# Local transformer: ScalarE lays the masks in PSUM, copies both halves of the turned probabilities and scales the MLP's rows

## What is computed

```python
qkv = x @ Wqkv                       # q, k, v, 16 heads x 64
q = l2norm(q) * qs; k = l2norm(k) * ksc
q = q * cos * scale + rotate_half(q) * sin * scale        # k likewise
mask = (it < jb) | (it > jb + w) | (jb == -1)
sim = einsum('bhwie,bhwje->bhwij', bq, bk2) * 8
attn = softmax(where(mask, -max, sim), -1)
x = x + (attn @ bv2) @ Wo            # then the MLP on shifted, normed rows:
x = x + (a * gelu(gate)) @ W2 + b2   # a, gate = norm(shifted x) @ W1 + b1
```

## Time and profile before

| | |
|---|---|
| median of 3 runs | 2441.62 us (2440.64 to 2445.67) |
| the profiled execution | 2439.11 us, of which the span is 2437.3 us |
| stretch of the 96 steps | about 540 to 2140 us of the span |
| busy in that stretch of 1600 us | PE 1532, DVE 1377, ACT 979, POOL 956 us |
| TensorE clock granted | 0.968 of full speed over all, 1.00 in that stretch |
| a half-layer with its MLP | about 137 us, e.g. 1176 to 1313 us |

### The profile page before, as it was taken

One profiled execution on the slowest core, in us unless ns is written; L12 is line 12 of the kernel. 1 busy time (PEld: TensorE's weight loads), 2 busy tenths in 40 slices (PEclk: granted clock), 3 DMA queues, 4 the chain that ended last, 5 costly groups with the idle time before them and its releaser, 6 DMA issues.

```text
span 2437.3 us, 83769 instructions
## 1 busy us (share of the span) xinstructions
PE 2257.1 (93%) x36453; PEld 1530.4 (63%) x36453; DVE 1855.8 (76%) x4174; ACT 1298.4 (53%) x2414; POOL 1154.0 (47%) x855
## 2 busy tenths in 40 slices
PE   8999899889999999999999999999999999979985
PEld 4567554446667666666667676666766676655564
DVE  5742588779988889798888889897888888756612
ACT  3524154355666666656566666656566666525332
POOL 1037300046666556565656556565656556410064
PEclk8989899899999999999999999999999999999898
DMA  9012200000111211121101211021111111130012
GB/s 297 31 31 41 59 1 1 5 27 20 41 29 37 68 33 31 35 68 37 42 20 37 69 45 33 20 68 37 42 26 31 33 46 33 34 109 2 21 37 77
DMA packets 63736, 106.92 MB, mean 44 GB/s; under 512 B 11700, under 2 KB 48831, under 8 KB 56844
## 3 DMA queue, kind: packets, MB, share of 16 engines
q1 hardware_dynamic: 57626, 93.00, 13.5%
q0 software_dynamic: 4736, 8.29, 1.7%
q10 hardware_dynamic: 1010, 0.29, 0.1%
HBM read 42.55 MB, written 13.24 MB: 23 GB/s over the span
## 4 chain that ended last, share of the span: by engine, by line
PE 62%; POOL 12%; DVE 11%; issue 10%; ACT 3%; DMA 2%; SPq 0%; POOLq 0%; ACTq 0%; DVEq 0%
PE ps L2213 10%; PE ps L2316 6%; PE ps L2295 5%; POOL mem L3007 5%; PE ps L2257 4%; PE ps L2234 4%; PE ps L2222 4%; PE ps L2272 3%; POOL mem L3020 3%; PE ps L2382 3%; PE ps L2368 2%; PE ps L2359 2%; PE ps L1196 2%; POOL mem L3014 2%; PE ps L1682 2%
## 5 line engine op out<-in xcount | busy, mean ns | idle before, releaser
L3007 POOL TENSOR_TENSOR mem<-mem 128x512 f32<-128x512 f32 x384 | 571.6, 1495 | 557.2 <-DVE mem L2524 554.0
L2213 PE MATMUL ps<-mem 128*128 128x512 f32 x768 | 380.8, 608 | 8.6 <-ACT mem L2811 3.4
L2839 ACT ACTIVATE mem<-ps 128x512 f32<-128x512 f32 x384 | 221.5, 603 | 155.7 <-PE ps L2234 155.1
L2818 ACT ACTIVATE mem<-ps 128x512 f32<-128x512 f32 x384 | 220.6, 597 | 144.1 <-PE ps L2213 107.3
L2519 DVE TENSOR_TENSOR mem<-ps,mem 128x512 f32<-128x512 f32 x384 | 258.5, 673 | 13.0 <-ACT mem L2818 13.0
L2524 DVE TENSOR_TENSOR mem<-ps,mem 128x512 f32<-128x512 f32 x384 | 261.2, 680 | 0.0
L2234 PEld LDWEIGHTS ps<-mem 128*128 128x128 f32 x1536 | 183.2, 142 | 114.9 <-issue 96.2
L2295 PEld LDWEIGHTS ps<-mem 64*64 64x64 f32 x12288 | 191.7, 135 | 79.7 <-issue 77.5
L2531 DVE TENSOR_REDUCE mem<-mem 128x16 f32<-128x1024 f32 x192 | 232.0, 1208 | 0.0
L3020 POOL TENSOR_TENSOR mem<-mem 128x1024 f32<-128x1024 f32 x95 | 180.7, 1902 | 82.0 <-DVE mem L2592 82.0
L2234 PE MATMUL ps<-mem 128*128 128x128 f32 x1536 | 212.0, 274 | 5.9 <-DVE mem L2564 3.1
(11 more groups left out here) (313 smaller groups left out, 4154.6 us busy)
## 6 DMA issues: line engine op xcount, KB each, us to landing
mem<-mem SPq DMA_DIRECT2D x48, 768.0 KB, 5.8
mem<-in_Wqkv SPq DMA_DIRECT2D x6, 1536.0 KB, 6.7
mem<-mem SPq DMA_DIRECT2D x36, 256.0 KB, 3.5
y<-mem SPq DMA_DIRECT2D x8, 512.0 KB, 6.2
mem<-in_W12T SPq DMA_DIRECT2D x8, 512.0 KB, 7.7
mem<-y SPq DMA_DIRECT2D x16, 256.0 KB, 4.9
mem<-in_L3W SPq DMA_DIRECT2D x16, 256.0 KB, 5.6
mem<-in_L2Wo SPq DMA_DIRECT2D x6, 512.0 KB, 7.0
```

The costliest lines, as they stand in the source:

```text
L2213: e.matmul(self.K.ps[:, o, :], self.columns(u, bb), self.K.l2[l % 2]["Wqkv"][:, 512 * i:512 * i + 512], start=True, stop=True, skip_group_ ...
L3007: e.tensor_tensor(t1[:, cols], t1[:, cols], self.T2[:, cols], ALU.add).then_inc(s("rotated"), 1)
```

## The change

The two mask matmuls of each step are gone. ACT writes the masks into banks 3 and 2 instead, with two copies (`a_mask`) during the step before; PE waits for a counter `seeds` and its score matmuls add onto what lies there. The transposes into bank 3 keep the same instruction with other accumulation flags. `a_mask` waits, for bank 3, until ACT's own copy of the transposes is done, and for bank 2 until DVE has read the third quarter of the rotation of `g + 3` (`rotated_half`). The second half of the turned probabilities is copied by ACT right behind the first, in 93 of 96 steps. The MLP's eight tiles of rows are scaled by ACT (`a_rows`) in 11 of 12 half-layers, between the second transposes' copy and the turn; DVE computes only the bias for it. The counter `bias_parts` of an earlier stage is now called `seeds` too.

```diff
-    BESIDE_ACT = {..., (1, 2): (("turn", 0),), ...}
+    BESIDE_ACT = {..., (1, 2): (("rows", 0), ("turn", 0)), ...}
@@ pe_by_feature
-            last = e.transpose(ps[:, o, 128 * c:128 * c + 128], self.T1[r % 2][k][:, h:h + 128], self.K.ident)
+            last = e.matmul(ps[:, o, 128 * c:128 * c + 128], self.T1[r % 2][k][:, h:h + 128], self.K.ident, start=c == 0,
+                            stop=True, is_transpose=True, skip_group_check=True)
@@ pe_scores
-        mask = self.K.maskb[:, 1 if u % 4 == 0 and g % 2 else 0, :]
         banks = self.SCORES
-        for odd in range(2):
-            after(e, self.freed[banks[odd]])
-            e.matmul(ps[:, banks[odd], :], self.K.identb, mask, start=True, stop=False, skip_group_check=True)
+        e.wait_ge(*s.at("seeds", 2 * g + 2))
@@ v_turned_p
+        if self.scalar_copies(g):        # g + 3 < self.NG
+            return
@@ v_norm
-        for i in range(8):
-            j = 8 * bp + i
-            e.tensor_scalar(K.XN[:, i, :], K.XN[:, i, :], K.mv[:, j, 0:1], K.rs[:, j:j + 1], ALU.subtract,
-                            ALU.mult).then_inc(s("mlp_rows"), 1)
+        if f + 1 < self.NF:
+            c = slice(8 * bp, 8 * bp + 8)
+            e.scalar_tensor_tensor(K.rt[:, c], K.mv[:, c, 0], -1.0, K.rs[:, c], ALU.mult, ALU.mult).then_inc(s("x_centred"), 1)
+        else:
+            ...
@@ scalar, even steps
                     self.a_by_feature(e, g + 2, 1)
                 if this:
+                    self.a_mask(e, g + 1, 1)
+                    self.a_mask(e, g + 1, 0)
                     self.a_beside(e, hl, w, 3)
@@ scalar, odd steps
                     self.a_values(e, u + 1, 3)
                 if placed:
+                    self.a_mask(e, g + 1, 0)
+                    self.a_mask(e, g + 1, 1)
+                if placed:
                     self.a_by_feature(e, g + 2, 2)
@@ new
+    def a_mask(self, e, g, odd):
+        K, s = self.K, self.s
+        if odd == 0:
+            if g + 1 < self.NG:
+                e.wait_ge(*s.at("placed", 4 * (g + 1) + 2))
+            else:
+                e.wait_ge(*s.at("lessened", 2 * g - 1))
+        elif g + 2 < self.NG:
+            e.wait_ge(*s.at("rotated_half", 4 * (g + 2) + 3))
+        else:
+            e.wait_ge(*s.at("lessened", 2 * g))
+        e.activation(K.ps[:, self.SCORES[odd], :], K.maskb[:, 1 if g % 8 == 1 else 0, :], ACT.Copy).then_inc(s("seeds"), 1)
+
+    def a_rows(self, e, f):
+        K, s = self.K, self.s
+        e.wait_ge(*s.at("x_centred", f + 3))
+        for i in range(8):
+            j = 8 * (f % 2) + i
+            e.activation(K.XN[:, i, :], K.XN[:, i, :], ACT.Identity, bias=K.rt[:, j:j + 1], scale=K.rs[:, j:j + 1]
+                         ).then_inc(s("mlp_rows"), 1)
@@ a_turned_p
+        if self.scalar_copies(g):
+            e.wait_ge(*s.at("p_turned", 2 * g + 2))
+            e.activation(view(self.PT[:, 1], "p c b h q -> p (c b h q)"), ps[:, self.TURN_P[1], :], ACT.Copy
+                         ).then_inc(s("p_cols_too"), 1)
```

More of the change, by code:

```diff
@@ L1467 @@
     LEAD = 3
-    TOTALS = dict(weight_sums=2, weight_totals=1, first_weights=1, second_weights=1, tap_rows=32, taps=3, bias_parts=1,
+    TOTALS = dict(weight_sums=2, weight_totals=1, first_weights=1, second_weights=1, tap_rows=32, taps=3, seeds=1,
                   normed=NT, ready_rows=NT, rows_turned=B, cols=B, up=NT, hidden_rows=NT, rounded=NT, rounded_turn=NT, cols2=NT,
@@ L1532, in v_steps @@
         e.wait_ge(v.sem, t)
-        e.tensor_copy(self.parts.bitcast(BF16)[three, 0:512], rest[three]).then_inc(s("bias_parts"), 1)
+        e.tensor_copy(self.parts.bitcast(BF16)[three, 0:512], rest[three]).then_inc(s("seeds"), 1)
         yield
@@ L1645, in tensor @@
         e.wait_ge(*s.at("taps", 3))
-        e.wait_ge(*s.at("bias_parts", 1))
+        e.wait_ge(*s.at("seeds", 1))
         for i in range(self.LEAD):
@@ L1967 @@
                   (5, 0): (("gate", 1),), (5, 2): (("down", 1),)}
-    BESIDE_ACT = {(1, 0): (("shift", 0),), (1, 1): (("guess", 0),), (1, 2): (("turn", 0),), (1, 3): (("turn", 1),),
+    BESIDE_ACT = {(1, 0): (("shift", 0),), (1, 1): (("guess", 0),), (1, 2): (("rows", 0), ("turn", 0)), (1, 3): (("turn", 1),),
                   (2, 2): (("gelu", 0),), (4, 1): (("turn_x", 0),), (4, 3): (("gelu", 1),), (6, 0): (("turn_x", 1),)}
     BESIDE_POOL = {(0, 0): (("kept", 0),), (4, 1): (("tables", 0),)}
-    TOTALS = dict(cleared=5, kept=32, kept_late=32, x_normed=NT, x_centred=2, x_turned=2 * NF, x_cols=4 * NF, tables=6 * DEPTH, qk=4 * NG, squared=4 * NG,
+    TOTALS = dict(cleared=5, kept=32, kept_late=32, x_normed=NT, x_centred=NF + 1, x_turned=2 * NF, x_cols=4 * NF, tables=6 * DEPTH, qk=4 * NG, squared=4 * NG,
                   guessed=NG, mlp_variance=NF, mlp_guessed=NF,
@@ L1975 @@
                   p_cols=NG, p_cols_too=NG, values_mm=4 * NU, values=4 * NU, values_shifted=16 * (2 * NU - NF),
-                  weighed=2 * NG, out_cols=2 * NG, projected=NU, attention_added=NU, shift_mm=NF, mlp_shifted=NF,
+                  seeds=2 * NG, weighed=2 * NG, out_cols=2 * NG, projected=NU, attention_added=NU, shift_mm=NF, mlp_shifted=NF,
                   mlp_kept=NF, mlp_rows=8 * NF, mlp_turned=2 * NF, mlp_cols=2 * NF, mlp_gated=6 * NF, mlp_up=6 * NF,
@@ L2598, in v_normalise, with scalar_copies @@
         self.fill()
+    def scalar_copies(self, g):
+        return g + 3 < self.NG
     def v_turned_p(self, e, g):
         s = self.s
+        if self.scalar_copies(g):
+            return
         e.wait_ge(*s.at("p_turned", 2 * g + 2))
@@ L2638, in v_norm @@
         e.wait_ge(K.v.sem, self.mlp_root)
-        for i in range(8):
-            j = 8 * bp + i
-            e.tensor_scalar(K.XN[:, i, :], K.XN[:, i, :], K.mv[:, j, 0:1], K.rs[:, j:j + 1], ALU.subtract,
-                            ALU.mult).then_inc(s("mlp_rows"), 1)
+        if f + 1 < self.NF:
[3 more added lines that the diff above has]
+            for i in range(8):
+                j = 8 * bp + i
+                e.tensor_scalar(K.XN[:, i, :], K.XN[:, i, :], K.mv[:, j, 0:1], K.rs[:, j:j + 1], ALU.subtract,
+                                ALU.mult).then_inc(s("mlp_rows"), 1)
     def v_gate(self, e, f, bb):
@@ L2689, in scalar @@
         self.a_by_feature(e, 1, 1)
+        self.a_mask(e, 0, 0)
         self.a_rotate(e, 2, 2)
         self.a_rotate(e, 2, 3)
+        self.a_mask(e, 0, 1)
         self.a_by_feature(e, 1, 2)
@@ L2789, in a_beside @@
                 self.a_mlp_guess(e, f)
+            elif what == "rows":
+                self.a_rows(e, f)
             elif what == "turn":
```

## The result

The changed kernel takes 2453.3 us, the kernel before it 2437.5 us in the same comparison (11 runs each). The ratio of the paired runs is 1.0089, 95% interval 1.0069 to 1.0110: slower by 21.7 us (the medians lie 15.8 us apart, the means 19.4). The forecast was 2437, a gain of 0.2%; the measured time is inside the range of 2412 to 2459, but the sign was wrong.

The account below looks back on a forecast made before the run. PE, busy 93% of the span, was taken to set the pace. Eleven half-layers (-3.4 us), the first (-0.9) and the last steps (-0.4) gave -4.7 on 2439.1: 2434.4, as median of runs 2437; range 2412 to 2459.

Parts of the forecast that it names:

- `w` = 2: Even step of a half-layer's eight (0 to 7); masks stand behind Gelu's tables on ACT: gain 0.26 us.
- `w` = 7: Odd step; ACT writes the masks ahead of its last two transposes' copies: gain 0.12 of 0.43 us.
- 3 and 4: Steps of a half-layer where ACT's copies end well ahead or masks fit before the Gelu table: gain 0.43 us each.
- `w` = 5: Odd step whose last copies on ACT come after the masks: loss 0.07 us.
- `w` = 6: Even step; masks ready 0.4 us earlier, taken again by ACT's later turned x at its head: 0.
- `w` = 1: Step with the MLP's rows, scaled on ACT ahead of a long queue: loss 0.96 us, bounds 0.7 and 1.6.
- the wait for the rows: In the step with the MLP's rows, the turn on PE waits some 2 us for ACT's scaled rows.
- The 1.5 to 2.5 us of PE idle: Expected sign in the trace: PE idle of this length ahead of the scores at `w` = 2.
- The second rival: Head of even steps: ACT's late copies delay guesses, squares, rotation and masks; 22 us slower, about 2459; chance 0.28.
- A step keeps its gain only if three other things are ready by then: At each step's scores: the rule limiting the direct return of 41.3 us from 96 mask pairs of 0.43 us.
- the last steps: End of the 96 steps, where no rotation follows: gain 0.4 us.
- It costs nothing while PE's product of rotation ends later than it: Odd steps: ACT's second probabilities' copy, ahead of the first rotation's square, is hidden by PE; otherwise 0.5 us a step.

Follow-up runs that it names:

- no_rows_ends: The changed kernel with the MLP's rows back on DVE and the masks of the first and last two steps back on PE: 1.0010 of the kernel before.
- ends_on_pe: The changed kernel with the masks of the first step and the last two back on PE: 1.0045 of the kernel before.
- the second pair: Two kernels with the MLP's rows back on DVE: all masks on ACT (1.0037), or those of the first and last two steps on PE (1.0010).
- The filler runs: Changed kernel, first and last two steps' masks on PE, plus matmuls that compute nothing in PE's waits: 1.0081 at two places, 1.0077 at one.
- both fillers: ends_on_pe plus idle matmuls, eight ahead of the turn of the MLP's rows and six ahead of the scores of `w` = 2: 1.0081 of before.
- warmed_turn: ends_on_pe plus only the eight idle matmuls ahead of the turn of the MLP's rows: 1.0077 of the kernel before.
- masks_most: Kernel before plus ACT's second probabilities' copy, and masks on ACT for five of eight steps (0, 1, 4, 5, 7) in eleven half-layers: 0.9989.

## Why the prediction was wrong in its sign

**The steps: right but for `w` = 2.** Five of eight came within 0.02 us of their numbers by the shortest sample (table above): `w` = 7 gained 0.12 and no more, 3 and 4 their whole pair, `w` = 5 lost 0.06. ACT's masks were 600 ns and 0.51 apart, against 0.63 and 0.52 assumed. `w` = 6 gained 0.18 where I had given all of 0.4 away again for ACT's late head. `w` = 1 lost 1.16, inside its bounds of 0.7 to 1.6. Only `w` = 2 was wrong in kind: instead of -0.26 it kept its shortest time and got a longer mean (16.88 to 17.14). The half-layer that I read for it had an instruction stall in this step, and ACT's copies stood 1.43 us ahead of the mask pair. In an undisturbed one it is 1.22 us, so that 0.05 us were to be had:

```profile
1241.98 0.43 PE L2257 MATMUL ps<-mem 64*32 64x64 f32 x26 [1.32 <-issue]
...
1796.21 1.09 ACT L2839 ACTIVATE mem<-ps 128x512 f32<-128x512 f32 x2
...
1797.43 0.60 PE L2250 MATMUL ps<-mem 128*128 128x512 bf16 x2
```

**The waits: right in the main.** POOL's wait at the turned probabilities went, but for 4.4 us, and ACT's rows and last copies took its place; the wait for the rows was longer than the 2 us I gave, 2.8 on average. The 1.5 to 2.5 us of PE idle ahead of the scores of `w` = 2 are not there.

**The second rival: the sign without the mechanism.** Its 22 us and its 2459 are near what was measured, but its place was the head of the even steps, which did not grow: `w` = 6 and 0 became shorter. That it came near is chance.

**The step that failed: "A step keeps its gain only if three other things are ready by then: both masks in PSUM, the banks, and in even steps the last transposes' copy."** I summed dependences at a fixed clock. The sum has no term for what waits do to the granted clock, none for the first scores, and it gives the last steps a gain. It came to -4.7 us; +21.7 was measured. The runs show two terms in its place. One is the clock in the inner steps: with nearly all their masks on ACT a kernel lacks some 17 us more of full-speed time (16.7 in no_rows_ends, 17.3 in ends_on_pe), an estimated 10 us at the 0.6 above, and 14 at most by the 0.81. The rows add nothing to it that shows: the falls stand at `w` = 1 with them and mostly about the scores of `w` = 2 without them. The other is the ends, 7 to 11 us (below). With the 0.3 us that eleven half-layers gave, where I had 3.4, that makes 16 to 21 us of the 21.7; each part is good to several us. I had myself put up to 2.5 us of PE idle into `w` = 1, and counted that as the length of the wait alone.

The Trainium skill ("TensorE: Matmul & The Clock Gate", "HAM oscillation — how this bites in real kernels") warns of a like case, whose gaps are waits for DMA: a kernel in which every tile has its gap runs part of every tile at the lower clock. The windows above agree in direction, 1.00 ahead of the wait and 0.65 after it. The page should have been a rival.

**The ends: mis-sized and with the wrong sign.** I gave the last steps -0.4 and the first scores no term. They cost some 11 us (ends_on_pe against the kernel after), 6.6 by the second pair. In the traces the last scores take 6.88 us from start to end in the kernel after, 2.84 in that before and 1.93 in ends_on_pe. Ahead of the first scores, and in the last steps where no rotation follows, PE has no work that covers ACT's masks; they lie on the path, and at the end they pushed the scores into the loads of the next stage.

**The rows: a sum that was known to lose.** The step's +0.96 was the largest term of my table, and it was bought with nothing: DVE's 2.14 us there ended a wait of up to 1.3 us that became one of 2.8 on average. It measured +1.16 to +1.25 by the step and 15.6 us by itself.

**The copy: "It costs nothing while PE's product of rotation ends later than it".** Right that it costs nothing, wrong that it brings nothing. In `w` = 7 DVE's copy stood between the turn and the product with the values, and taking it away gave 0.59 us a half-layer. The kernel after doesn't show this gain, since in `w` = 7 ACT's masks take it again (15.26 against 14.79).

**Open.** The price of the lower clock rests on a fit over traces and on few single half-layers, and no run changes the clock alone. The filler runs don't settle it. With both fillers the lack went from 17.3 to 2.5 us, and the run grew by 7.7 us where their own 1.3 us a half-layer would have made 14: that gives back 0.45 us per us. But warmed_turn lacked 9 us less than ends_on_pe and was no faster. Between the two first traces the mean steps don't differ (135.63 and 135.45), though one lacks 24 us more of clock over the steps, 10 of them in the half-layers that the means are taken from; the kernel before had lost as much in stalls and waits at that time, and in its second execution it hadn't (134.94). Not tried: a kernel in which only the place of the instructions in memory changes, which would say whether the stalls hang on that.

## What to carry to other kernels

Before work is taken off the engine that sets the pace, ask what it covered: where it goes, a wait may come to stand in its place, and the time that the lower clock takes behind such waits has to be set against what it gives. Take it away only in the steps where nothing is late behind it, here two of eight (0.9940 with the copy), rather than in nearly all (1.0010 with the copy). Read the mean granted clock of every timed run beside its time, but ask of the trace in which stretch it is lost. And look at the first and the last step of a pipeline by themselves: here three steps of 96 cost about as much as the clock.

## What the hardware did that was not expected

- ACT's write of 128 x 512 bf16 into PSUM takes 600 ns, pair 1.11 us; its copy of 512 columns out of PSUM takes 584 to 598. The Trainium skill ("ScalarE: Activation LUTs", "Step-by-step: what each stage is for") calls the write to PSUM the faster one. Against the 631 ns that the line through the Exp rows gives for an SBUF source (an estimate from the earlier trace rows) it is 31 ns faster; against the PSUM to SBUF copy there is no gain.
- TensorE's instruction stalls come at much the same places in two executions of a program (23 matmuls ahead of the end of the burst of `w` = 2 in half-layer 3 in both traces of the kernel before, 0.74 and 1.01 us), many of them in the last 40 matmuls of a burst of 128, and last 0.2 to 2.4 us; beside a load of weights some last 4.5 to 5.8 us. Over the steps they add up to 13.9 us (copy alone) to 32.5 us (masks_most).
- The granted clock fell behind single waits within a step: to a window mean of 0.65 behind the wait of 2.76 us for the rows, and of 0.76 behind a stall of 2.10 us that itself followed a wait of 1.60 us.
- Executions of one kernel differ by up to 1.2%: the kernel before took 2424 to 2454 us over all comparisons, and 2427 to 2454 us within one of them.
